# Graph network layer on one core: one gathered tile in 32 is built from SBUF columns instead

## The chip, the core and the metric

The kernel runs on one core of a Trainium2 chip. The core has five engines that run their own instruction streams side by side and wait for each other on semaphores: TensorE (PE, matrix products into PSUM banks), VectorE (DVE), ScalarE (ACT), GpSimd (POOL) and SyncE (SP, which only issues DMAs here). The metric is the time of one execution on the device in microseconds (us), the median of several runs.

## The reference

`x` holds 12500 nodes of 64 features. 200000 edges, sorted by `dst`, have a source and a destination node and 32 features each. What is computed:

```python
msg_in = concatenate([nodes[row], nodes[col], edge_features], axis=-1)   # 64 + 64 + 32
messages = relu(msg_in @ mW1 + mb1) @ mW2 + mb2                         # 128 hidden, 64 out
aggregated = segment_sum(messages, col, num_segments=12500)
upd_in = concatenate([nodes, aggregated], axis=-1)
update = relu(upd_in @ uW1 + ub1) @ uW2 + ub2
out = layernorm(x + update)                                             # over the 64 features
```

`row` is `src`, `col` is `dst`. All data are float32.

## The kernel before

**Tables.** The hidden layer of a message is a sum of three products, and two of them depend on a node alone. So TensorE first multiplies all nodes with the source rows of `mW1` (`src_table`, 12800 x 128, in DRAM) and with the destination rows plus `mb1` (`dst_table`, in DRAM). `xc` is a resident tile of [128, 12800]: its rows 0 to 63 hold `x` transposed, one node a column; its rows 64 to 127 later hold counts.

**Groups and laps.** The edges are worked off in tiles of 128, four tiles to a group of 512 (`TPG`), 391 groups, and `UNROLL` = 8 groups to a lap, `ITERS` = 49 laps. On each engine lap 0 and the last lap are written out, and between them runs a loop (L413, 25 laps), then a second loop (L418, 22 laps) in which each lap also does one of 25 chunks of the node update and the layer norm. `k` is the number of a group in its lap. For a group g:

- GpSimd (`gather`, L223) issues four indirect DMAs. Each fetches for the 128 edges of a tile the rows of `src_table` into `ag[:, k, ...]`, by the indices in `slot_idx`. It may run 8 groups ahead: it waits for `s_idx` of group g - 8.
- SyncE loads the features of the edges into rows 96 to 127 of `picks` (L232) and 96 rows of `dst_table`, a window from a base that it reads into a register, into `picked` (L238). Since the edges are sorted, the destinations of a group lie in such a window.
- VectorE makes the one-hot `oh` of each edge's place in the window two groups ahead (`one_hot`, L299), adds the gathered rows to the product (`add_source`, L312), copies the indices of group g + 8 into `slot_idx` (`next_indices`, L318), and adds the sums of group g - 2 into `agg_t` (L328) and the counts into `xc` (L329), at columns from a register.
- TensorE transposes the one-hot of group g + 1 (L247), multiplies `picks` with `picked` (`hidden`, L260), and sums the messages of group g - 1 by window place (`aggregate`, L270, L274).
- ScalarE copies the transposed one-hot of group g + 1 out of PSUM (L285) and applies the ReLU to `hid` (L291).

The window bases of a lap are loaded into registers once a lap by one load of 8 values on VectorE and one on SyncE (`window_bases`, L333). Its first element is 8i for SyncE and 8i - 2 for VectorE in lap i.

**What sets the order.** Each engine's instructions stand in the order in which they are written, k by k; semaphores that count groups tie the engines together. In `add_source` VectorE waits for three things, the first of which is the gathered rows:

```python
wait(dve, s_gathered[k], (lap + 1) * 16 * TPG - 16 * missing)
wait(dve, s_h, g + 1)
wait(dve, s_agg, g - 1)
```

In the laps of the second loop VectorE has steps of a chunk behind k = 1, 2, 5 and 6 (`dve_c2`, `dve_stack`, `dve_center`, `dve_variance`, `dve_normalize`), ScalarE at k = 3 and 6, TensorE at k = 2, 3 and 5. Ahead of the laps stands a prologue of some 100 us, in which the tables are made, and in which VectorE works out windows that SyncE stores to DRAM and loads back spread over the partitions.

Of the kernel before, what the change touches and what calls it, by code (L numbers as in the profile page):

```python
# [6 lines left out]
D = 64  # L7
# [31 lines left out]
TSTEPS = -(-BLOCKS // TB)  # L39
ASLOTS = UNROLL  # L40
# [6 lines left out]
def build(nc, x_rows, x_t, src_first, src_all, dst_groups, dst_tiles, edge_t,  # L47
# [3 lines left out]
    bf16 = mybir.dt.bfloat16  # L51
    ALU = mybir.AluOpType
# [6 lines left out]
    with ctx:  # L59
# [15 lines left out]
        lag_dram = dram("window_lag", (GROUPS,))  # L75
        agg_dram = dram("agg_rows", (AGG_ROWS, AGG_W))
# [46 lines left out]
        oh = sb("oh", [P, RING, TPG * WIN])  # L123
        hid = sb("hid", [P, 2, TPG * DH])
# [3 lines left out]
        dst_g_real = resid[0:GROWS, GPP * GE:2 * GPP * GE]  # L128
        base_all = resid[:, 2 * GPP * GE:2 * GPP * GE + GROUPS]
# [34 lines left out]
        s_flag = sem("s_flag")  # L164
        s_rel = sem("s_rel")
# [12 lines left out]
        s_window = [sem(f"s_window{i}") for i in range(RING)]  # L178
        s_oh = sem("s_oh")
# [34 lines left out]


# [35 lines left out]
        def hidden(pe, g, k, lap):  # L251
# [6 lines left out]
            wait(pe, s_pre, g - 1)  # L258
            for j in range(TPG):
                last = nc.tensor.matmul(ps_h[q][:, j * DH:(j + 1) * DH], picks[:, r, j * P:(j + 1) * P],  # L260
                                        picked[:, r, :], start=True, stop=True)
# [25 lines left out]
        def relu(g, k):  # L287
# [16 lines left out]
        def add_source(g, k, lap):  # L304
# [4 lines left out]
            wait(dve, s_gathered[k], (lap + 1) * 16 * TPG - 16 * missing)  # L309
# [240 lines left out]
        def general_vector():  # L550
            dve = nc.vector
            dst_table_stored(dve)
            dve.wait_ge(s_src, 16)
# [203 lines left out]
        def _(pool):  # L757
# [14 lines left out]
            def windowed():  # L772
                with pool.Fori(1, ITERS - 1) as i:  # L773
                    for k in range(UNROLL):
                        gather(pool, i * UNROLL + k, k)
                for g in range((ITERS - 1) * UNROLL, G_END):
                    gather(pool, g, g % UNROLL, min(TPG, T_END - g * TPG))
# [4 lines left out]
        def _(sp):  # L782
            sp.dma_start(slot_idx[:, :], src_first).then_inc(s_first, 16)
            sp.dma_start(dst_g, dst_groups).then_inc(s_dstg, 16)
            sp.dma_start(w_dst[:, :], mw1[D:2 * D, :]).then_inc(s_wdst, 16)
# [9 lines left out]
            sp.wait_ge(s_scratch, 64)  # L795
# [62 lines left out]
        def _(act):  # L858
# [11 lines left out]
            def windowed():  # L870
                dst_table_stored(act)
                copy_oh(0, 0)

                def lap(i, c):
                    for k in range(UNROLL):
# [7 lines left out]
                        if exists(g):  # L883
                            relu(g, k)
# [193 lines left out]
```

## Time and profile before

| | |
|---|---|
| time, median of 3 runs | 2049.36 us (2049.04 to 2050.01) |
| profiled execution, its own time | 2048.59 us |
| span in its profile | 2046.8 us |
| busy: GpSimd / TensorE matmul / VectorE / ScalarE | 1480 / 1439 / 872 / 563 us |
| gathers | 1563, 946 ns each |
| laps of the first loop / of the second | 25 / 22 |

The span is the stretch that the profile covers; the 1.8 us between it and the execution's own time lie outside. The busy time of an engine is the sum of its instructions; its sequencer, which reads the instructions, works out addresses in registers, loads registers and issues DMAs, is shown apart, as DVEq, ACTq, POOLq and SPq, and isn't counted as busy. Idle time before an instruction is put down to what ended it, behind an arrow; "issue" stands for time in which the engine waited for nothing that the profile shows.

### The profile page before, as it was taken

How to read it: one execution, taken by the hardware profiler on the slowest of the kernel's cores; microseconds unless marked ns; L12 is line 12 of the kernel's file. 1: busy time of each engine (PE TensorE's matmuls, PEld its weight loads, DVE VectorE, ACT ScalarE, POOL GpSimd, SP SyncE). 2: the span in 40 equal slices, each digit the busy share in tenths (PEclk: the TensorE clock that was granted, in tenths of full speed). 3: DMA queues.
4: the chain of work that ended last, by engine and by line, in shares of the span. 5: the costliest groups of instructions: out<-in, count | busy, mean ns of one | idle time of the engine just before them, and what ended most of it. 6: DMA issues, size and time to landing. Idle time of an engine off the chain costs nothing.

```text
span 2046.8 us, 34700 instructions
## 1 busy us (share of the span) xinstructions
PE 1438.8 (70%) x10080; PEld 1316.0 (64%) x10080; DVE 871.9 (43%) x2220; ACT 562.8 (27%) x929; POOL 1480.1 (72%) x1572
## 2 busy tenths in 40 slices
PE   7986666776666766766677767677677767667675
PEld 7976666666656666665666656566566656566664
DVE  3353333333333343333333444445444444444444
ACT  2332222222222222222222333233333333333332
POOL 0567777777777777777777777777777777777774
PEclk9997777777787687778876878787888778877877
DMA  8732323322232233223222223233223322232321
GB/s 212 206 100 79 80 78 77 82 78 78 80 80 78 78 80 80 77 78 81 79 76 72 80 78 82 75 81 79 76 78 80 80 75 81 78 80 75 82 78 46
DMA packets 167585, 173.49 MB, mean 85 GB/s; under 512 B 65654, under 2 KB 129433, under 8 KB 167209
## 3 DMA queue, kind: packets, MB, share of 16 engines
q0 software_dynamic: 50016, 102.53, 19.4%
q1 hardware_dynamic: 104088, 63.37, 11.2%
q10 hardware_dynamic: 13458, 7.31, 1.6%
q8 instruction: 12, 0.20, 0.0%
q14 instruction: 11, 0.08, 0.0%
HBM read 156.74 MB, written 16.31 MB: 85 GB/s over the span
## 4 chain that ended last, share of the span: by engine, by line
POOL 68%; issue 24%; PE 5%; POOLq 1%; DMA 1%; DVE 0%; ACT 0%; SPq 0%; ACTq 0%; DVEq 0%
POOL ag L223 68%; PE bank L367 4%; DMA xc<-x_t 1%; PE bank L260 0%; POOLq L209 0%; PE bank L270 0%; POOLq L220 0%; POOLq L773 0%; PE bank L634 0%; DMA ag<-src_table,slot_idx 0%; DMA dst_table<-picks 0%; DMA picks<-edge_t 0%; PE bank L247 0%; PE bank L640 0%; PE bank L274 0%
## 5 line engine op out<-in xcount | busy, mean ns | idle before, releaser
L223 POOL DMA_INDIRECT ag<-src_table,slot_idx x1563 | 1479.1, 946 | 543.8 <-issue 485.3
L270 PE MATMUL bank<-oh,hid 128*128 128x96 f32 x3128 | 533.5, 326 | 414.2 <-DVE xc L329 370.5
L270 PEld LDWEIGHTS bank<-oh,hid 128*128 128x128 f32 x3128 | 479.9, 234 | 472.7 <-ACT hid L291 425.0
L312 DVE TENSOR_TENSOR hid<-bank,ag 128x512 f32<-128x512 f32 x391 | 270.3, 691 | 886.6 <-DMA ag<-src_table,slot_idx 751.0
L260 PE MATMUL bank<-picked,picks 128*128 128x128 f32 x3128 | 582.5, 345 | 3.7 <-DMA picks<-edge_t 3.1
L291 ACT ACTIVATE hid<-hid 128x512 f32<-128x512 f32 x391 | 245.7, 628 | 1164.8 <-DVE hid L312 1164.8
L260 PEld LDWEIGHTS bank<-picked,picks 128*128 128x128 f32 x3128 | 520.7, 252 | 6.9 <-issue 3.3
L285 ACT ACTIVATE picks<-bank 96x512 f32<-96x512 f32 x391 | 226.2, 579 | 181.8 <-PE bank L247 132.3
L299 DVE TENSOR_TENSOR oh<-iota,rel 128x384 f32<-128x384 f32 x391 | 218.0, 558 | 117.9 <-PE bank L274 61.1
L247 PE MATMUL bank<-ident_bf,oh 128*96 128x128 bf16 x1564 | 193.6, 260 | 53.2 <-DVE oh L299 52.6
L247 PEld LDWEIGHTS bank<-ident_bf,oh 128*96 128x96 bf16 x1564 | 147.4, 155 | 103.4 <-DVE oh L299 65.7
L274 PE MATMUL bank<-oh,ones_bf 128*128 128x96 bf16 x1564 | 156.5, 230 | 0.0
L274 PEld LDWEIGHTS bank<-oh,ones_bf 128*128 128x128 bf16 x1564 | 144.4, 123 | 1.2
L634 PE MATMUL bank<-agg_t,w_pad 128*128 (+2 forms) x50 | 50.5, 1119 | 90.3 <-DVE resid L655 90.3
L328 DVE TENSOR_TENSOR agg_t<-bank,agg_t 128x96 f32 x391 | 100.6, 257 | 15.6 <-PE bank L274 1.8
L329 DVE TENSOR_TENSOR xc<-bank,xc 64x96 f32 x391 | 102.2, 261 | 5.9 <-issue 0.5
L318 DVE COPY slot_idx<-src_idx 128x4 int32 (+1 forms) x384 | 66.0, 172 | 57.6 <-DVE hid L312 57.3
L634 PEld LDWEIGHTS bank<-agg_t,w_pad 128*128 128x128 f32 x50 | 12.7, 313 | 94.8 <-issue 89.3
L367 PE MATMUL bank<-w_src,xc 64*128 64x128 f32 x200 | 43.0, 418 | 12.3 <-DMA xc<-x_t 12.3
L367 PEld LDWEIGHTS bank<-w_src,xc 64*128 64x128 f32 x200 | 42.7, 330 | 12.3 <-issue 12.3
L640 PE MATMUL bank<-xc,u 128*128 (+2 forms) x50 | 27.4, 634 | 26.0 <-DVE xc L663 26.0
L367 PE MATMUL bank<-w_dst,xc 64*128 64x128 f32 x200 | 43.0, 418 | 0.8 <-ACT ag L378 0.8
(55 smaller groups left out, 349.4 us busy)
## 6 DMA issues: line engine op xcount, KB each, us to landing
picks<-edge_t SPq DMA_DIRECT2D x391, 64.0 KB
ag<-src_table,slot_idx POOLq DMA_INDIRECT x1563
picked<-dst_table SPq DMA_DIRECT2D x391, 48.0 KB
src_table<-ag SPq DMA_DIRECT2D x25, 256.0 KB, 3.5
dst_table<-picks SPq DMA_DIRECT2D x17, 256.0 KB, 2.6
xc<-x_t ACTq DMA_DIRECT2D x4, 800.0 KB, 16.0
resid<-x_rows SPq DMA_DIRECT2D x24, 128.0 KB
out<-resid ACTq DMA_DIRECT2D x24, 128.0 KB
```

Source lines behind the costliest of these rows:

```text
L223: pool.indirect_dma_start(out=ag[:, k, j * DH:(j + 1) * DH], out_offset=None, in_=src_table, in_offset=bass.IndirectOffsetOnAxis(ap=slot_i ...
L247: last = nc.tensor.matmul(ps_o[q][0:WIN, j * P:(j + 1) * P], half[:, j * WIN:(j + 1) * WIN], ident_bf[:, :], start=True, stop=True)
L260: last = nc.tensor.matmul(ps_h[q][:, j * DH:(j + 1) * DH], picks[:, r, j * P:(j + 1) * P], picked[:, r, :], start=True, stop=True)
L270: nc.tensor.matmul(ps_a[q][:, 0:WIN], hid[:, q, j * DH:(j + 1) * DH], oh[:, r, j * WIN:(j + 1) * WIN], start=(j == 0), stop=(j == TPG - 1))
L274: last = nc.tensor.matmul(ps_a[q][:, WIN:2 * WIN], ones_bf[:, :], half[:, j * WIN:(j + 1) * WIN], start=(j == 0), stop=(j == TPG - 1))
L285: act.activation(picks[0:WIN, r, :], ps_o[q][0:WIN, :], ACT.Copy).then_inc(s_oht, 1)
L291: act.activation(hid[:, q, :], hid[:, q, :], ACT.Relu).then_inc(s_relu, 1)
L299: dve.tensor_tensor(oh[:, r, :].rearrange("p (j w) -> p j w", w=WIN), iota[:, None, :].to_broadcast(grid), rel[:, ds(g * TPG, TPG)][:, :, ...
L312: dve.tensor_tensor(hid[:, q, :], ps_h[q][:, :], ag[:, k, :], ALU.add).then_inc(s_pre, 1)
L328: dve.tensor_tensor(to, ps_a[q][:, 0:WIN], to, ALU.add)
L329: dve.tensor_tensor(cnt, ps_a[q][D:P, WIN:2 * WIN], cnt, ALU.add).then_inc(s_added, 1)
L367: last = nc.tensor.matmul(banks[n % 4][:, b * DH:(b + 1) * DH], xc[0:D, at:at + P], w[:, :], start=True, stop=True)
```

## The change

Group k = 5 of each lap from 1 on loses the gather of its last tile. In its place the sources' columns of `x` are collected in SBUF: `own_x` is [64, 128], one edge a column. Of its 128 columns 16 are filled in each of the 8 groups before, from k = 5 of the lap ahead on: 8 by VectorE with `tensor_copy`, 8 by ScalarE with a copying activation. Each column is `xc[0:64, node]`, and `node` is in a register that one load of 8 values fills, from `own_row`, one partition of SBUF in which the sources of these tiles stand as 16-bit integers. TensorE multiplies `own_x` with the source weights into the same PSUM columns on top of the product of L260, once both engines have reported their columns. `add_source` of that group then adds 384 columns only, and the ReLU is two activations, one straight from PSUM. In the prologue the indices come in by a DMA, are cast by VectorE, stored to DRAM and loaded back into `own_row`.

```diff
+        def own_indices(eng, lap, at, n):
+
+            return nc.values_load_multi_w_load_instructions(
+                own_row[0:1, ds(lap * P + at, n)], engines=(eng,), min_val=0, max_val=N_NODES - 1,
+                skip_runtime_bounds_check_because="an index of a node")[1]
+        def own_part(k, lap):
+
+            return lap + (k >= OWN_K), (k - OWN_K) % UNROLL * OWN_N
+        def fills_own(lap):
+
+            return not isinstance(lap, int) or 0 < lap < ITERS
+        def own_columns_dve(k, lap):
+
+            dve = nc.vector
+            lap, at = own_part(k, lap)
+            if fills_own(lap):
+                for n, node in enumerate(own_indices(ET.DVE, lap, at, OWN_DVE)):
+                    last = dve.tensor_copy(own_x[:, at + n:at + n + 1], xc[0:D, ds(node, 1)])
+                last.then_inc(s_own_dve, 1)
+        def own_columns_act(k, lap):
...
+                for n, node in enumerate(own_indices(ET.Activation, lap, at, OWN_N - OWN_DVE)):
+                    last = act.activation(own_x[:, at + n:at + n + 1], xc[0:D, ds(node, 1)], ACT.Copy)
+                last.then_inc(s_own_act, 1)
...
+            if own:
+                pe.wait_ge(s_own_dve, lap * UNROLL)
+                pe.wait_ge(s_own_act, lap * UNROLL)
+                last = nc.tensor.matmul(ps_h[q][:, OWN_AT:], own_x[:, :], w_src[:, :], start=False, stop=True)
             last.then_inc(s_h, 1)
...
+            if has_own(k, lap):
+                act.activation(hid[:, q, OWN_AT:], ps_h[q][:, OWN_AT:], ACT.Relu)
+                act.activation(hid[:, q, 0:OWN_AT], hid[:, q, 0:OWN_AT], ACT.Relu).then_inc(s_relu, 1)
+                return
...
-            dve.tensor_tensor(hid[:, q, :], ps_h[q][:, :], ag[:, k, :], ALU.add).then_inc(s_pre, 1)
+            w = OWN_AT if has_own(k, lap) else TPG * DH
+            dve.tensor_tensor(hid[:, q, 0:w], ps_h[q][:, 0:w], ag[:, k, 0:w], ALU.add).then_inc(s_pre, 1)
...
-                        gather(pool, i * UNROLL + k, k)
+                        gather(pool, i * UNROLL + k, k, TPG - (k == OWN_K))
...
-            sp.wait_ge(s_scratch, 64)
+            sp.wait_ge(s_own_h, 1)
+            sp.dma_start(own_dram, own_h).then_inc(s_scratch, 16)
+            sp.wait_ge(s_scratch, 80)
+            sp.dma_start(own_row[:, :], own_dram.rearrange("(o t) e -> o (t e)", o=1)).then_inc(s_own_row, 16)
...
                         if exists(g):
-                            relu(g, k)
+                            relu(g, k, i)
+                        own_columns_act(k, i)
...
                             add_window(g - 2, (k - 2) % UNROLL, bases[k])
+                        own_columns_dve(k, i)
                         if c is not None:
                             if k == 1:
                                 dve_c2(c)
```

On VectorE, inside the first loop, a group ended before with the two adds of `add_window`, and the one-hot and `add_source` of the next group followed (ISA is a register operation of the sequencer, `oh` the one-hot, `hid` what goes into the ReLU):

```order
L328 ISA [waits s_added,s_agg]
L328 TENSOR_TENSOR agg_t<-bank,agg_t 128x96
L329 ISA
L329 TENSOR_TENSOR xc<-bank,xc 64x96
L299 ISA [waits s_agg]
L299 TENSOR_TENSOR oh<-iota,rel 128x384
L312 TENSOR_TENSOR hid<-bank,ag 128x512 [waits s_agg,s_h,s_gathered1]
```

In the changed kernel the same place reads as follows (L395 and L396 are the old L328 and L329); the last two rows stand seven times more before the one-hot, now L365:

```order
L395 ISA [waits s_added,s_agg]
L395 TENSOR_TENSOR agg_t<-bank,agg_t 128x96
L396 ISA
L396 TENSOR_TENSOR xc<-bank,xc 64x96
L234 ISA
L234 TENSOR_LOAD own_row
L256 ISA
L256 COPY own_x<-xc 64x1
```

So a load and 8 pairs of a register operation and a copy stand between a group's last add and the next one-hot, in every group.

On ScalarE, in the first loop, a group was the copy of the one-hot and the ReLU:

```order
L209 REGISTER_ALU
L285 ACTIVATE picks<-bank 96x512 [waits s_h,s_oht_mm]
L291 ACTIVATE hid<-hid 128x512 [waits s_pre]
L209 REGISTER_ALU
L285 ACTIVATE picks<-bank 96x512 [waits s_h,s_oht_mm]
```

Now, at k = 5, where the ReLU is split (the last two rows again stand seven times more):

```order
L225 REGISTER_ALU
L347 ACTIVATE picks<-bank 96x512 [waits s_h,s_oht_mm]
L354 ACTIVATE hid<-bank 128x128 [waits s_pre]
L355 ACTIVATE hid<-hid 128x384
L234 ISA
L234 TENSOR_LOAD own_row
L266 ISA
L266 ACTIVATE own_x<-xc 64x1
```

The next copy of a one-hot out of PSUM thus stands behind a load and 8 activations.

On TensorE, at k = 5 in the first loop, before:

```order
L260 MATMUL bank<-picked,picks 128x128 [waits s_window1,s_pre,s_edge1,s_oht]
L260 MATMUL bank<-picked,picks 128x128 x3
L270 MATMUL bank<-oh,hid 128x96 [waits s_added,s_relu]
L270 MATMUL bank<-oh,hid 128x96 x3
L274 MATMUL bank<-oh,ones_bf 128x96 x4
```

And after:

```order
L318 MATMUL bank<-picked,picks 128x128 [waits s_window1,s_pre,s_edge1,s_oht]
L318 MATMUL bank<-picked,picks 128x128 x3
L323 MATMUL bank<-w_src,own_x 128x128 [waits s_own_act,s_own_dve]
L332 MATMUL bank<-oh,hid 128x96 [waits s_added,s_relu]
L332 MATMUL bank<-oh,hid 128x96 x3
L336 MATMUL bank<-oh,ones_bf 128x96 x4
```

One matmul more, with a wait for both engines that fill `own_x`, ahead of the aggregation of the group before.

## Rows read from the trace of the kernel before

**Rows 1.** The page: chain that ended last by engine, the gathers' group.

```profile
POOL 68%; issue 24%; PE 5%; POOLq 1%; DMA 1%; DVE 0%; ACT 0%; SPq 0%; ACTq 0%; DVEq 0%
...
L223 POOL DMA_INDIRECT ag<-src_table,slot_idx x1563 | 1479.1, 946 | 543.8 <-issue 485.3
```

**Rows 2.** Timeline of GpSimd: start us, us, engine, line, instruction, idle before.

```profile
620.71 0.94 POOL L223 DMA_INDIRECT ag<-src_table,slot_idx  x1 [0.30 <-issue]
621.96 0.94 POOL L223 DMA_INDIRECT ag<-src_table,slot_idx  x1 [0.30 <-issue]
```

**Rows 3.** VectorE's loop branches: ns min/median/max, first to last start us.

```profile
L413 DVEq FUSED_REGOPS  x25: 85/85/85, 125.2 to 1071.8; - x25
...
L413 DVEq COMPARE_BRANCH  x25: 50/56/67, 152.7 to 1111.5; - x25
...
L418 DVEq COMPARE_BRANCH  x22: 50/56/69, 1152.1 to 1993.9; - x22
```

**Rows 4.** Line L312 in 140 to 1100, 1120 to 2000, 1994 to 2047 us.

```profile
  DMA ag<-src_table,slot_idx: 488.0, 192
...
  DMA ag<-src_table,slot_idx: 241.1, 134
  issue: 124.9, 42
...
  DMA ag<-src_table,slot_idx: 14.4, 6
```

**Rows 5.** Register loads of L333: whole run, prologue's end, last stretch.

```profile
L333 DVEq TENSOR_LOAD <-base_row x50: 529/1846/1865, 102.3 to 2029.1; - x50
L333 SPq TENSOR_LOAD <-base_row x49: 521/525/701, 102.2 to 1974.8; - x49
...
L333 DVEq TENSOR_LOAD <-base_row x1: 844/844/844, 102.3 to 102.3; - x1
...
L333 DVEq TENSOR_LOAD <-base_row x2: 529/1188/1847, 1994.0 to 2029.1; - x2
```

**Rows 6.** Timeline of VectorE: a lap's end, then a whole group.

```profile
671.96 0.26 DVE L329 TENSOR_TENSOR xc<-bank,xc 64x96 f32 x1
674.42 0.57 DVE L299 TENSOR_TENSOR oh<-iota,rel 128x384 f32<-128x384 f32 x1 [2.20 <-PE bank L274]
...
1025.39 0.69 DVE L312 TENSOR_TENSOR hid<-bank,ag 128x512 f32<-128x512 f32 x1 [2.93 <-DMA ag<-src_table,slot_idx]
...
1026.71 0.26 DVE L329 TENSOR_TENSOR xc<-bank,xc 64x96 f32 x1
1027.00 0.56 DVE L299 TENSOR_TENSOR oh<-iota,rel 128x384 f32<-128x384 f32 x1
```

**Rows 7.** Register operation ahead of that L329; small independent instructions in the prologue.

```profile
L329 DVEq FUSED_REGOPS  x1: 65/65/65, 1026.5 to 1026.5; - x1
...
15.18 0.15 DVE L924 TENSOR_TENSOR spread<-dst_mx,base_f 98x4 f32<-98x4 f32 x1
15.25 0.15 DVE L928 TENSOR_TENSOR lag<-lag_f,base_f 98x4 f32<-98x4 f32 x1
```

**Rows 8.** Groups of ScalarE, shapes kept apart: busy us, mean ns, idle before.

```profile
L291 ACT ACTIVATE hid<-hid 128x512 f32<-128x512 f32 x391 | 245.7, 628 | 1164.8 <-DVE hid L312 1164.8
L285 ACT ACTIVATE picks<-bank 96x512 f32<-96x512 f32 x391 | 226.2, 579 | 181.8 <-PE bank L247 132.3 <-DMA dst_table<-picks 30.0 <-DVE resid L713 19.2
...
L693 ACT ACTIVATE dst_i<-resid 128x128 f32<-128x128 f32 x1 | 0.3, 309 | 0.8 <-DVE resid L687 0.8
```

**Rows 9.** A matmul of 64 rows; VectorE's wait for its first bank.

```profile
L367 PE MATMUL bank<-w_src,xc 64*128 64x128 f32 x200 | 43.0, 418 | 12.3 <-DMA xc<-x_t 12.3
...
58.26 0.69 DVE L388 TENSOR_TENSOR picks<-bank,b_rows 128x512 f32<-128x512 f32 x1 [18.10 <-PE bank L367]
```

**Rows 10.** Lines L318 and L223, whole run: duration ns min/median/max.

```profile
L318 DVE COPY slot_idx<-src_idx x384: 169/170/394, 108.3 to 1993.5; 128x4 int32 x188, 128x4 int32<-128x4 int32 x4
...
L223 POOL DMA_INDIRECT ag<-src_table,slot_idx x1563: 940/944/1285, 59.4 to 2023.8; - x196
```

More of the change, by code:

```diff
@@ L39 @@
 TSTEPS = -(-BLOCKS // TB)
+OWN_K = 5
+OWN_N = P // UNROLL
+OWN_DVE = OWN_N // 2
+OWN_J = TPG - 1
+OWN_AT = OWN_J * DH
 ASLOTS = UNROLL
@@ L213, in upper_halves, with has_own, gathered_of @@
             return ap.bitcast(bf16).rearrange("p (n two) -> p n two", two=2)[:, :, 1]
+        def own_indices(eng, lap, at, n):
+            return nc.values_load_multi_w_load_instructions(
+                own_row[0:1, ds(lap * P + at, n)], engines=(eng,), min_val=0, max_val=N_NODES - 1,
+                skip_runtime_bounds_check_because="an index of a node")[1]
+        def has_own(k, lap):
+            return k == OWN_K and not (isinstance(lap, int) and lap == 0)
+        def own_part(k, lap):
[10 more added lines that the diff above has]
+        def own_columns_act(k, lap):
+            act = nc.scalar
+            lap, at = own_part(k, lap)
+            at += OWN_DVE
+            if fills_own(lap):
+                for n, node in enumerate(own_indices(ET.Activation, lap, at, OWN_N - OWN_DVE)):
+                    last = act.activation(own_x[:, at + n:at + n + 1], xc[0:D, ds(node, 1)], ACT.Copy)
+                last.then_inc(s_own_act, 1)
+        def gathered_of(k, lap):
+            return 16 * TPG + lap * 16 * (TPG - (k == OWN_K))
         def gather(pool, g, k, tiles=TPG):
@@ L258, in hidden @@
             wait(pe, s_pre, g - 1)
+            own = has_own(k, lap)
             for j in range(TPG):
                 last = nc.tensor.matmul(ps_h[q][:, j * DH:(j + 1) * DH], picks[:, r, j * P:(j + 1) * P],
-                                        picked[:, r, :], start=True, stop=True)
+                                        picked[:, r, :], start=True, stop=not (own and j == OWN_J))
+            if own:
+                pe.wait_ge(s_own_dve, lap * UNROLL)
+                pe.wait_ge(s_own_act, lap * UNROLL)
+                last = nc.tensor.matmul(ps_h[q][:, OWN_AT:], own_x[:, :], w_src[:, :], start=False, stop=True)
             last.then_inc(s_h, 1)
@@ L285, in copy_oh, with relu @@
             act.activation(picks[0:WIN, r, :], ps_o[q][0:WIN, :], ACT.Copy).then_inc(s_oht, 1)
-        def relu(g, k):
+        def relu(g, k, lap):
             act = nc.scalar
@@ L308, in add_source @@
             missing = G_END * TPG - T_END if isinstance(g, int) and g == G_END - 1 else 0
-            wait(dve, s_gathered[k], (lap + 1) * 16 * TPG - 16 * missing)
+            wait(dve, s_gathered[k], gathered_of(k, lap) - 16 * missing)
             wait(dve, s_h, g + 1)
             wait(dve, s_agg, g - 1)
-            dve.tensor_tensor(hid[:, q, :], ps_h[q][:, :], ag[:, k, :], ALU.add).then_inc(s_pre, 1)
+            w = OWN_AT if has_own(k, lap) else TPG * DH
+            dve.tensor_tensor(hid[:, q, 0:w], ps_h[q][:, 0:w], ag[:, k, 0:w], ALU.add).then_inc(s_pre, 1)
         def next_indices(g, k):
```

22 lines of the change are left out of this document (20 added, 2 removed).

## The prediction

> **What bounds the kernel now.** Read the page's chain that ended last first: GpSimd holds 68% of it and "issue" another 24%, and GpSimd's gathers are busy for 1479 of 2046.8 us and preceded by 485 us of "issue", 0.3 us each [rows 1]. The timeline of GpSimd shows the gathers at an even pitch, 620.71, 621.96, with no wait on anybody [rows 2]. The laps of VectorE take (1111.5 - 152.7) / 24 = 39.95 us without the update and (1993.9 - 1152.1) / 21 = 40.09 us with it [rows 3]; a lap of 8 groups has 32 gathers, and 39.95 / 32 = 1.248 us is the pitch of the timeline. So today's lap is a lap of gathers.
>
> The second question is how far behind the next engine is. The idle time of VectorE before `add_source` (L312) is the slack: in 24 laps without the update it waits 488.0 us for gathered rows, 20.3 us a lap; in 22 laps with it 241.1 us, 11.0 us a lap, and another 124.9 us that no gather ended ("issue": waits inside the chain of the update, which stay) [rows 4]. Taking one gather out of a lap is worth 1.248 us; whatever VectorE gets in return has to fit into these two numbers.
>
> **What is removed.** One gather in each of the laps 1 to 48: 48 x 1.248 = 59.9 us, if GpSimd stayed the bound. That is the most that the change can give: 2048.6 - 59.9 = 1989 us. A lap of gathers becomes 31 x 1.248 = 38.7 us.
>
> **What VectorE gets.** After the window add of every group (L396 in the new file) it loads 8 node numbers into registers and copies 8 columns, each from an address in a register. So 8 loads and 64 copies a lap, 384 groups in all (3 in lap 0, 8 in each of the laps 1 to 47, 5 in lap 48).
>
> *The load.* VectorE has a load of 8 registers already, once a lap (`window_bases`, L333): 50 of them, median 1846 ns, and the only shorter ones are a load of 6 registers (844 ns) and one of 2 (within 529 to 1847 ns, so 529) [rows 5]. The sequencer does nothing else meanwhile: at a lap's end L329 is over at 672.22 and the next one-hot starts at 674.42, where it follows 0.03 us behind in the middle of a lap [rows 6]. SyncE loads the same 8 numbers in 525 ns [rows 5]. The two differ in the engine and in where the load begins: element 8i for SyncE, 8i - 2 for VectorE. The new loads are VectorE's, begin at a multiple of 16 and read 2-byte numbers, so both ends are possible: 0.52 us and 1.85 us. I take 1.85: same engine, same number of registers, and its median and its longest are 19 ns apart; the 6 registers at 844 ns, which begin at element 0, are what speaks against it.
>
> *The copies.* Each has a register operation in front of it, 65 ns for the one that stands before L329 today, and small independent instructions start 70 ns behind each other although each runs 150 ns [rows 7]. So 0.06 + 0.07 = 0.13 us a column, 1.04 us for 8. Lower bound 0.07 (register operations cost nothing), upper bound 0.20 (a copy runs 0.17 us, as L318 does [rows 10], and the next waits for its end and 0.03 us).
>
> *The sum for one group*: 0.07 us register operation ahead of the load, 1.85 load, 1.04 columns, 0.13 for the register operation and dispatch of the following one-hot, which today hides beside L329, and minus 0.30 us, since the sequencer is done with L329 (1026.5 + 0.065) well before the engine is (1026.97) and starts the load meanwhile [rows 6, 7]: 2.79 us. A lap: 8 x 2.79 = 22.3 us against a slack of 20.3 and 11.0 us. It doesn't fit. VectorE becomes the bound:
> - a lap without update: 39.95 - 20.3 + 22.3 = 41.95 us (from the other side: a group without waits on others runs from 1025.39 to 1027.00 + 0.56, 2.2 us [rows 6], 8 x (2.2 + 2.79) + 2.2 for the lap's own load = 42.1);
> - a lap with update: 40.09 - 11.0 + 22.3 = 51.4 us.
>
> **What else moves.** ScalarE gets the same load and 8 activations. Its two instructions of a group take 579 + 628 ns, an activation of 128 columns 309 ns [rows 8], of which some 0.1 us are the columns (628 - 309 = 319 ns for 384 more); with 1.85 us for the load and 0.2 us a column a group is 1.2 + 1.85 + 1.6 = 4.65 us, under VectorE's 2.2 + 2.79 = 4.99, so it hides behind VectorE even at that upper end. TensorE gets one matmul a lap (64 rows, at 418 ns for one of its two passes [rows 9], so under 0.9 us) that waits for the columns of the group before; VectorE's next one-hot (0.56 us) runs meanwhile, so at most 0.3 us of a lap is exposed, and I count nothing. ScalarE's split ReLU costs one more start, some 0.2 us, off the path. In the prologue SyncE waits for one more small store before it loads the window tables, and VectorE reads them; VectorE stands idle there for 18 us until TensorE has its first bank [rows 9], which covers it. GpSimd's wait for free indices is 8 groups behind and costs nothing while gathers are not late; once VectorE is the bound, GpSimd waits there, which is where the removed 60 us go.
>
> **The sum.** Lap 0 ends at 125.2 us on VectorE [rows 3], plus 3 x 2.79 = 8.4: 133.6. Then 25 x 41.95 = 1048.8, 0.9 for the entry into the second loop, 22 x 51.4 = 1130.8. The last lap and the tail took 2046.8 - 1993.9 = 52.9 us; 5 x 2.79 = 14.0 us more stand against 14.4 us of waits for gathers in it [rows 4], so 52.9 again. Total 2367.0 us of span; the profiled execution is 1.8 us longer than its span (2048.59 to 2046.8) and 0.8 us under the median, so about **2369 us**, 15.6% slower.
>
> **A rule against the rows.** The trace has loads at 0.52 and 1.85 us [rows 5]. The Trainium skill ("Runtime: NRT & Kernel Launch", section Instruction fetch mechanics) says that a register load (the runtime's own, from HBM) costs about 200 ns for each register even in bulk; 8 would be an estimated 1.6 us, which is nearer to VectorE's row and disagrees with SyncE's, and with 1.6 the sum above would come to some 2275 us, still slower.
>
> **Rivals.**
> (a) *The load is as quick as SyncE's (0.52 us).* A group costs 0.07 + 0.52 + 1.04 + 0.13 - 0.30 = 1.46 us, a lap 11.7 us. That fits into 20.3 (the lap is then the gathers' 38.7) and nearly into 11.0 (40.09 - 11.0 + 11.7 = 40.8): -1.25 x 25 + 0.7 x 22 = -16, so 2033 us, and 1989 us if the columns take 0.07 each as well. This is the side on which the kernel gets faster; with columns at 0.13 it decides at a load of about 0.6 us. For it: SyncE's 49 loads. Against it: none of VectorE's is that short with over 2 registers.
> (b) *The load is in between, 1.0 us*, as a line through VectorE's 529 ns for 2 and 844 ns for 6 registers gives for 8. A group costs 1.94 us, a lap 15.5: still 38.7 without the update, but 44.6 with it: 2048.6 - 31 + 22 x 4.5 + 4 = 2121 us, slower.
> (c) *The columns don't overlap* (0.20 each): 0.56 us more in each of 384 groups, 2369 + 215 = 2584 us.
> (d) *The copies stop GpSimd.* VectorE's small copy L318 runs 384 times beside the gathers; its median is 170 ns, its shortest 169, and the gathers stand at 940 to 944 ns in half their records [rows 10]: no sign that either waits. If each of the 8 copies held a gather for the 0.15 us it runs, the pitch would be 1.248 + 2 x 0.15 = 1.55 us, the lap without the update 31 x 1.55 = 48.0, and the total 2369 + 25 x 6 = 2520 us. The Trainium skill ("SBUF — State Buffer", Who interferes with whom) has this rule: a copy of VectorE between SBUF tensors in a 2-port mode and a GpSimd instruction shut each other out completely; by it the time is this rival's, and the trace shows no sign of it for L318.
> (e) *Nothing of the kind: 48 gathers less and all the rest hidden*, 1989 us. It needs (a) and the cheap columns together and is counted with (a).
>
> **How the numbers follow.** Chances: forecast 0.61 (load 1.6 to 2.1 us), (a) 0.16, (b) 0.14, (c) 0.06, (d) 0.03. The forecast's own range comes from the load at 1.6 (384 x 0.25 = 96 us less), from the columns at 0.10 (384 x 0.24 = 92 less) and, upward, from the 0.30 us of overlap that may not be there (384 x 0.30 = 115 more): 2185 to 2485 us. The range of 8 in 10 takes in (b) and the slower half of (a), whose forecast is 2033: 2025 to 2485. It leaves out the quick half of (a), (c) and (d). What a measurement can tell from no change here is about 0.2%, 4 us; (a) lies on both sides of it where the load is near 0.6 us. Faster 0.15, same 0.04, slower 0.81.
>
> **What would show it.** In the profile after: the register loads that the changed kernel adds on VectorE, with their duration (1.85 us confirms the main term, 0.5 us overturns it); idle time of GpSimd that VectorE's `slot_idx` copy ends, beside the even 0.3 us of "issue" that is all it has now; VectorE's wait for gathers in L379 gone to nearly nothing in both loops; the laps at 42 and 51 us by the loop's branches; copies of 64x1 starting 0.13 us apart. The forecast is wrong if the loads are short, or if ScalarE or TensorE, not VectorE, is what the others wait for in the laps with the update: then the second number, 51.4, is too low, since waits of one engine within the update's chain would add up with those of the other.

## The result, and the profile after

The changed kernel takes 2390.3 us (median of 4 runs, 2387.3 to 2392.8), the kernel before 2049.7 us in the same session (2049.0 to 2050.1): a ratio of 1.166, 95% interval 1.164 to 1.168. The forecast was 2369 us. The profiled execution took 2387.3 us, 2385.5 of them span. The runs of experiments 5 and 6 were taken on two other chips, on which the kernel before itself takes 2672 and 2670 us: no conclusion on the time of a kernel is drawn from them, only on the duration of single instructions.

The page of the changed kernel, first the busy time of each engine, then the two groups that answer to [rows 1] and to the added columns:

```profile
PE 1600.0 (67%) x10176; PEld 1449.1 (61%) x10176; DVE 1232.8 (52%) x5293; ACT 924.3 (39%) x4050; POOL 1464.9 (61%) x1524
...
L280 POOL DMA_INDIRECT ag<-src_table,slot_idx x1515 | 1463.9, 966 | 861.4 <-issue 405.1
L256 DVE COPY own_x<-xc 64x1 f32 x3072 | 366.7, 146 | 653.8 <-issue 653.8
```

48 gathers are gone (1515 for 1563), and GpSimd's idle time has grown from 543.8 to 861.4 us. VectorE is busy for only 52% of the span, but before its column copies it stands "idle" for 653.8 us: that is not a wait for anybody, it is the register load, which the page doesn't count as busy. One line of the register loads, one of the copies, from their line views (duration ns min/median/max):

```profile
L234 ACTq TENSOR_LOAD <-own_row x384: 1707/1716/2078, 118.8 to 2358.4; - x192
L234 DVEq TENSOR_LOAD <-own_row x384: 1823/1828/2189, 119.1 to 2357.6; - x192
...
L256 DVEq FUSED_REGOPS  x3072: 46/46/53, 120.9 to 2360.2; - x192
```

384 loads of 1.83 us on VectorE, 384 of 1.72 us on ScalarE. A group of VectorE, to be held against [rows 6] (timeline; start us, us, instruction):

```profile
700.69 0.26 DVE L396 TENSOR_TENSOR xc<-bank,xc 64x96 f32 x1
702.65 0.95 DVE L256 COPY own_x<-xc 64x1 f32 x8 [1.70 <-issue]
703.59 0.56 DVE L365 TENSOR_TENSOR oh<-iota,rel 128x384 f32<-128x384 f32 x1
704.18 0.69 DVE L379 TENSOR_TENSOR hid<-bank,ag 128x512 f32<-128x512 f32 x1
```

From L396 to the next one-hot it is 2.90 us; it was 0.29 us (1026.71 to 1027.00). So a group costs VectorE 2.61 us more. There is no idle time before L379: the gathered rows are there. The line view of L379 gives 3.9 us of waits in 192 groups of the first loop (for L323, the added matmul), where [rows 4] had 488.0 us for gathers. The loops' branches on VectorE, to be held against [rows 3]:

```profile
L480 DVEq FUSED_REGOPS  x25: 85/85/85, 131.2 to 1121.0; - x25
L480 DVEq COMPARE_BRANCH  x25: 50/56/67, 172.3 to 1162.0; - x25
...
L485 DVEq COMPARE_BRANCH  x22: 50/56/69, 1216.7 to 2332.5; - x22
```

The first loop (L480) takes (1162.0 - 172.3) / 24 = 41.24 us a lap, before 39.95; the second (L485), which carries the update, (2332.5 - 1216.7) / 21 = 53.13 us, before 40.09. The tail is 2385.5 - 2332.5 = 53.0 us as it was. Of the 339 us of span, 6 come from lap 0 (131.2 for 125.2), 45 from the first loop (125.2 to 1111.5 before, 131.2 to 1162.0 now; 14 of them from its first lap, which took 27.5 us and now takes 41.1 like the rest) and 288 from the second (to 1993.9 before, to 2332.5 now).

### The profile page after: what moved, and what is told of

The parts are those of the page before. It is cut to its first block and busy times, and to the rows that moved or that the text cites. A ratio compares the mean times of both kernels' runs of the same rounds, so it can differ in the third digit from the quotient of the medians.

```text
span 2385.5 us, 48801 instructions
## 1 busy us (share of the span) xinstructions
PE 1600.0 (67%) x10176; PEld 1449.1 (61%) x10176; DVE 1232.8 (52%) x5293; ACT 924.3 (39%) x4050; POOL 1464.9 (61%) x1524
## 5 line engine op out<-in xcount | busy, mean ns | idle before, releaser
L280 POOL DMA_INDIRECT ag<-src_table,slot_idx x1515 | 1463.9, 966 | 861.4 <-issue 405.1
L256 DVE COPY own_x<-xc 64x1 f32 x3072 | 366.7, 146 | 653.8 <-issue 653.8
L332 PE MATMUL bank<-oh,hid 128*128 128x96 f32 x3128 | 599.8, 356 | 102.6 <-ACT hid L357 80.0
L332 PEld LDWEIGHTS bank<-oh,hid 128*128 128x128 f32 x3128 | 565.1, 271 | 131.5 <-ACT hid L357 117.7
L318 PE MATMUL bank<-picked,picks 128*128 128x128 f32 x3128 | 610.9, 357 | 22.7 <-ACT picks L347 16.4
L318 PEld LDWEIGHTS bank<-picked,picks 128*128 128x128 f32 x3128 | 541.1, 260 | 34.1 <-issue 24.5
L266 ACT ACTIVATE own_x<-xc 64x1 f32 x3072 | 344.2, 193 | 489.1 <-issue 489.1
L357 ACT ACTIVATE hid<-hid 128x512 f32<-128x512 f32 x343 | 215.3, 628 | 494.7 <-DVE hid L379 492.7
L379 DVE TENSOR_TENSOR hid<-bank,ag 128x512 f32<-128x512 f32 (+1 forms) x391 | 263.7, 674 | 198.7 <-issue 174.1
L365 DVE TENSOR_TENSOR oh<-iota,rel 128x384 f32<-128x384 f32 x391 | 219.6, 562 | 126.4 <-issue 68.1
L323 PE MATMUL bank<-w_src,own_x 64*128 64x128 f32 x96 | 30.3, 407 | 126.6 <-DVE own_x L256 125.7
L395 DVE TENSOR_TENSOR agg_t<-bank,agg_t 128x96 f32 x391 | 100.9, 258 | 14.2 <-issue 3.5
L396 DVE TENSOR_TENSOR xc<-bank,xc 64x96 f32 x391 | 102.0, 261 | 5.4
L708 PE MATMUL bank<-xc,u 128*128 (+2 forms) x50 | 44.5, 990 | 87.5 <-DVE xc L731 87.5
L323 PEld LDWEIGHTS bank<-w_src,own_x 64*128 64x128 f32 x96 | 18.7, 242 | 136.9 <-DVE own_x L256 136.9
```

The lines of the kernel that those rows point to most:

```text
L256: last = dve.tensor_copy(own_x[:, at + n:at + n + 1], xc[0:D, ds(node, 1)])
L266: last = act.activation(own_x[:, at + n:at + n + 1], xc[0:D, ds(node, 1)], ACT.Copy)
L280: pool.indirect_dma_start(out=ag[:, k, j * DH:(j + 1) * DH], out_offset=None, in_=src_table, in_offset=bass.IndirectOffsetOnAxis(ap=slot_i ...
L332: nc.tensor.matmul(ps_a[q][:, 0:WIN], hid[:, q, j * DH:(j + 1) * DH], oh[:, r, j * WIN:(j + 1) * WIN], start=(j == 0), stop=(j == TPG - 1))
L365: dve.tensor_tensor(oh[:, r, :].rearrange("p (j w) -> p j w", w=WIN), iota[:, None, :].to_broadcast(grid), rel[:, ds(g * TPG, TPG)][:, :, ...
L379: dve.tensor_tensor(hid[:, q, 0:w], ps_h[q][:, 0:w], ag[:, k, 0:w], ALU.add).then_inc(s_pre, 1)
```

## The experiments

The question on top: is it VectorE's time, as forecast, and of that the load? The rival: the gathers, since the changed kernel waits for them by other counts and gathers three tiles of a group instead of four. Then: why does one load of 8 registers take 0.52 us and another 1.83?

**1. Eight kinds of load in the kernel before.** Each group of the first loop gets one more load on VectorE and on ScalarE, and one copy that uses its last value.

```
+ load_a8(i): base_row[0:1, ds(i * UNROLL, 8)]          L344
+ load_m8(i): base_row[0:1, ds(i * UNROLL - 2, 8)]      L347
+ load_a6(i): base_row[0:1, ds(i * UNROLL, 6)]          L350
+ load_a4(i): base_row[0:1, ds(i * UNROLL, 4)]          L353
+ load_a2(i): base_row[0:1, ds(i * UNROLL, 2)]          L356
+ load_a1(i): base_row[0:1, ds(i * UNROLL, 1)]          L359
+ load_h8(i): row16[0:1, ds(i * 2 * UNROLL, 8)]         L362
+ load_s8(i): base_row[0:1, 8:16]                       L365
```

> The kernel before with one register load more in each group of the first loop, on VectorE and on ScalarE, each followed by one small copy that uses its last value: 8 int32 from element 8i, 8 int32 from 8i-2, 4, 2, 1 int32 from 8i, 8 int16 from a multiple of 16, 6 int32 from 8i, 8 int32 from a fixed element. What decides how long a load of 8 takes on VectorE? If it is the start (theory S), the aligned int32 load takes 0.5 to 0.9 us and 8i-2 takes 1.85, and ScalarE shows the same split. If it is the engine and the number of registers (theory N, a cost per register), all loads of 8 take about 1.85 us on VectorE, 4 about 1.1, 2 about 0.6, 1 about 0.35. If the 2-byte type alone is slow (theory T), the int32 loads are short and the int16 one takes 1.83 us. Time of the whole: these loads cost VectorE some 8 x 1.6 = 13 us a lap against 20 us of slack, so 2049 us under N and less load under S; any rise over 0.5% would mean that loads also slow GpSimd.

The line views, VectorE's loads and one of ScalarE:

```profile
L344 DVEq TENSOR_LOAD <-base_row x25: 594/598/607, 127.8 to 1100.6; - x25
L347 DVEq TENSOR_LOAD <-base_row x25: 1854/1859/1872, 130.5 to 1105.8; - x25
L350 DVEq TENSOR_LOAD <-base_row x25: 825/828/837, 148.5 to 1130.8; - x25
L353 DVEq TENSOR_LOAD <-base_row x25: 344/347/352, 134.4 to 1110.7; - x25
L356 DVEq TENSOR_LOAD <-base_row x25: 535/539/549, 137.2 to 1115.9; - x25
L359 DVEq TENSOR_LOAD <-base_row x25: 310/314/317, 139.9 to 1120.9; - x25
L362 DVEq TENSOR_LOAD <-base_row x25: 1830/1834/1852, 143.8 to 1126.0; - x25
...
L344 ACTq TENSOR_LOAD <-base_row x25: 537/550/565, 127.3 to 1100.1; - x25
```

The engine makes little difference (598 and 550 ns); the type and the start decide, so theories S and T hold together and N falls. One int32 costs 314 ns, two 539, but four from a multiple of 16 bytes 347 and eight 598. The same eight int32 from 8 bytes before such a multiple cost 1859, and eight int16 from a multiple of 16 bytes 1834. All of it agrees, to some 30 ns, with one reading: a load takes its int32 in fours as long as each four begin at a multiple of 16 bytes, and anything else value by value, at (1834 - 314) / 7 = 217 ns each. Six are then four together and two alone, 347 + 2 x 225 = 797 ns, measured 828 (225 ns is what the second of two costs). So the 844 ns that the prediction took for "6 registers" is such a sum, and SyncE's 525 against VectorE's 1846 in [rows 5] is the start (8i against 8i - 2), not the engine. The Trainium skill ("Runtime: NRT & Kernel Launch", section Instruction fetch mechanics) gives some 200 ns for each register of the runtime's own loads from HBM even in bulk: the loads value by value, here from SBUF, agree (217 ns), the ones in fours (87 ns a register for four, 75 for eight) don't.

The run took 2072.3 us against 2050.3 (one run), though the loads, 6.9 us a lap on VectorE, fit almost three times into its slack of 20.3. Experiment 4 comes back to that.

**2. The gather isn't left out.** The fourth tile of the group k = 5 of each lap is gathered too, and not used; the waits count as in the kernel before. Everything else stays.

```
- return 16 * TPG + lap * 16 * (TPG - (k == OWN_K))
+ return (lap + 1) * 16 * TPG
...
- gather(pool, i * UNROLL + k, k, TPG - (k == OWN_K))
+ gather(pool, i * UNROLL + k, k)
...
```

> The changed kernel, but all 32 tiles are gathered as before, and the gathered rows of the 32nd tile are not used. If VectorE is the bound (my theory), the gather given back costs nothing: 2390 us within 0.3%. If the time of the changed kernel still hangs on GpSimd (rival), it rises by up to 60 us, to 2450.

2389.3 us (4 runs; 1.166 times the kernel before, 1.164 to 1.168), against 2390.3 for the changed kernel: the 48 gathers are worth nothing. GpSimd has 1563 gathers again and still stands idle until VectorE's indices are written:

```profile
L280 POOL DMA_INDIRECT ag<-src_table,slot_idx x1563: 938/944/1338, 58.8 to 2327.2; - x196
...
  DVE slot_idx L385: 343.8, 262
```

In the changed kernel that row is 399.4 us in 296 waits: 56 of the 60 us that were taken off GpSimd went into this wait.

**3. One column of eight.** The loads stay, each engine copies one column a group; the other 14 of 16 are left out and hold zeros, so the product of the tile is made with a mostly empty own_x.

```
- for n, node in enumerate(own_indices(ET.DVE, lap, at, OWN_DVE)):
+ for n, node in list(enumerate(own_indices(ET.DVE, lap, at, OWN_DVE)))[:1]:
...
- for n, node in enumerate(own_indices(ET.Activation, lap, at, OWN_N - OWN_DVE)):
+ for n, node in list(enumerate(own_indices(ET.Activation, lap, at, OWN_N - OWN_DVE)))[:1]:
```

> The changed kernel with its loads, but only the first of the 8 columns of each group is copied on VectorE and on ScalarE; the other columns hold zeros. A group gets 1.83 + 0.2 - 0.3 us and one column: 1.8 us, 14.5 us a lap. Without the update that fits (38.7 us a lap); with it 29.1 + 14.5 + 3 us = 46.6 where the changed kernel has 53.1. Sum: 2049 - 31 + 22 x 6.5 = 2160 us; 2095 if the 3 us that the changed kernel's update laps take above my sum come from the columns. If a load hides beside other work better than I think, it is at 2000.

```profile
L480 DVEq COMPARE_BRANCH  x25: 50/56/67, 163.2 to 1106.6; - x25
...
L485 DVEq COMPARE_BRANCH  x22: 50/56/69, 1154.2 to 2090.8; - x22
```

2139.7 us (1.044, 1.042 to 1.045), between the two times expected. The first loop is down to 39.31 us a lap, the second to 44.60. Seven columns less are 7 x 0.115 = 0.81 us a group, 6.4 us a lap. The second loop gains 8.5 us by it, 2.1 more than VectorE spends on the columns; experiment 7 shows where they come from.

**4. No load.** The copies take their addresses from the loop's counter, so no index is read, and the columns are those of other nodes.

```
- return nc.values_load_multi_w_load_instructions(
-     own_row[0:1, ds(lap * P + at, n)], engines=(eng,), ...)[1]
+ return [lap * P + (at + m) for m in range(n)]
```

> The changed kernel without the register loads on VectorE and ScalarE: the address of a column comes from the lap's register and a constant, so each column still has its register operation and its copy, but the columns are those of other nodes. If the load is the main cost (my theory), VectorE gets 8 columns x 0.115 us and about 0.2 us more a group, 9 us a lap, which fits into 20.3 and 11.0 us: the laps are the 38.7 us of 31 gathers, total 1990 to 2010 us. If the columns or the coupling of three engines are what costs (rival), it stays over 2200 us.

```profile
POOL 68%; issue 23%; PE 6%; DMA 1%; POOLq 1%; DVE 1%; ACT 0%; SPq 0%; DVEq 0%; ACTq 0%
...
L278 POOL DMA_INDIRECT ag<-src_table,slot_idx x1515 | 1474.2, 973 | 529.3 <-issue 467.4
```

2030.6 us (0.990, 0.9885 to 0.9918). Without the load 360 us are gone, the chain is GpSimd's again, and this kernel, which doesn't compute the right columns, is 1% faster than the kernel before. Load and columns don't add up: all columns without the load are worth -20 us against the kernel before, the loads with one column +89, both together +341, since each alone fits, or nearly, into the slack of the laps. But it is slower than the 1990 to 2010 us expected, and this is the second place where laps of gathers are too long: the loops' branches give 40.04 and 39.23 us for 31 gathers, where 31 x 1.248 is 38.7. That is experiment 1's riddle again. The mean gather has grown from 946 to 973 ns, and the timeline says which:

```profile
635.40 0.94 POOL L278 DMA_INDIRECT ag<-src_table,slot_idx  x1 [0.30 <-issue]
636.51 0.56 DVE L363 TENSOR_TENSOR oh<-iota,rel 128x384 f32<-128x384 f32 x1 [2.45 <-issue]
636.64 1.24 POOL L278 DMA_INDIRECT ag<-src_table,slot_idx  x1 [0.30 <-issue]
```

This gather starts while the one-hot runs and ends 0.81 us after the one-hot's end (637.07 to 637.88) instead of 0.94 after its own start. All 142 gathers of this run that start 0.045 to 0.37 us into a one-hot are held like it and take 1.006 us or more. Over this run the gathers are 44 us longer than 944 ns each, in the kernel before 4 us, and the difference is what 2030.6 lies above 2050.3 - 59.9 = 1990.4. In the kernel before VectorE waits for the gathers in L312, which keeps its one-hot mostly at a fixed place between two of them, and only 20 gathers are over a microsecond; here 160 are. The loads of experiment 1 loosen the same lock: 136 gathers are over a microsecond there, and all are 27 us longer instead of 4, which is about its 22 us. The column copies do nothing of the kind: none of the 163 gathers that start inside one is over a microsecond. At 638.72 to 639.59 eight copies run across the start of a gather of 0.94 us.

```profile
638.72 0.87 DVE L254 COPY own_x<-xc 64x1 f32 x8
639.44 0.94 POOL L278 DMA_INDIRECT ag<-src_table,slot_idx  x1 [0.30 <-issue]
```

**5. The one-hot reads iota from PSUM.** Theory: the gather is held because the one-hot has both its inputs in SBUF. The Trainium skill has that rule ("SBUF — State Buffer", Who interferes with whom): such an instruction contends with a GpSimd instruction that reads SBUF; one with at most one SBUF input, outside VectorE's 2-port modes, doesn't. The edit, here on the kernel of experiment 4, and once more in experiment 6:

```
- iota = sb("iota", [P, WIN])
+ iota = banks[6][:, 0:WIN]
```

> The kernel without register loads (e3), with the one-hot's iota moved from SBUF into the PSUM bank that nothing uses, so that the one-hot has one SBUF input instead of two. The kernel without loads had laps of 40.04 us without the update, where 31 gathers at 1.248 us are 38.7; its gathers that start while a one-hot runs take 1.25 to 1.34 us instead of 0.94. If it is the one-hot that holds them through its second SBUF input (my theory), they are all back at 0.94 us here, the laps at 38.7, and the total near 1995 us. If it is VectorE's column copies that hold them (rival, the fourth of the prediction), the gathers stay as they are, and the total stays at 2030.

The time, 2720.3 us against 2672.3 for the kernel before, says nothing on it, for the reason given with the result. The gathers say it: their mean is 946 ns for 973, at the same number of columns. The last two kernels of experiment 6, on one chip, differ in nothing but the place of iota, and there the count is clean: of the gathers that start 0.045 to 0.37 us into a one-hot, all 126 take over 1 us with iota in SBUF (`e11_first_loop_int32`), and of 110 with iota in PSUM (`e12_first_loop_int32_psum`) none takes more than 0.947. One of the latter, 0.17 us into the one-hot:

```profile
485.16 0.56 DVE L371 TENSOR_TENSOR oh<-bank,rel 128x384 f32<-128x384 f32 x1 [2.28 <-remote]
485.33 0.94 POOL L286 DMA_INDIRECT ag<-src_table,slot_idx  x1 [0.30 <-issue]
```

The trace of experiment 4 has a pair of its own in the update: of the 16 gathers that start inside `resid<-resid,stat` (L753, both inputs in SBUF) 14 take over 1 us, of the 17 that start inside `resid<-bank,resid` (L746, one input in PSUM, the same 128x256) none. The mechanism is shown, and the rule agrees with it; what moving iota would give in time isn't shown.

**6. The tile left out in the first loop alone, with int16 and with int32 indices, and with iota in PSUM.** The laps with the update gather all 32 tiles again; own_row then needs to hold some half as many numbers and is kept as int32 in two of the three. Each was run in two sessions, on two chips.

```
- with pool.Fori(1, ITERS - 1) as i:
+ with pool.Fori(1, UPD_LAP) as i:
...
+ with pool.Fori(UPD_LAP, ITERS - 1) as i:
+     for k in range(UNROLL):
+         gather(pool, i * UNROLL + k, k)
...
- own_row = sb("own_row", [1, ITERS * P], i16)
+ own_row = sb("own_row", [1, (UPD_LAP + 1) * P], i32)
```

> The changed kernel with the own tile in the 25 laps of the first loop only; the laps with the update gather all 32 tiles and have no columns. VectorE is still the bound of the first loop (41.2 us a lap), 50 us behind the kernel before at its end, of which GpSimd's lead of 6 more groups gives back some 30: about 2070 us. If the second loop's cost in the changed kernel came from something left behind by the first, it would be well above.

> The same with the node numbers as int32, 8 from a multiple of 16 elements. By the measured loads this one takes 0.6 us instead of 1.83, so a group costs VectorE 1.4 us more than before instead of 2.6, 11 us a lap against 20.3 of slack: the first loop is bound by 31 gathers again. Without any hold of GpSimd 38.7 us a lap and 2018 us in all; with gathers held by one-hots as in the kernel without loads (1.35 us a lap) 2050. If the type of the number were not what decides the load, 2070 as with int16.

> The same with the iota in PSUM. If the one-hot's second SBUF input is what holds the gathers, the first loop has laps of 38.7 us and the total is 2049 - 31 = 2018 us, faster than before by 1.5%. Rival: no effect of the iota's place, same time as the run with int32 alone.

> The changed kernel with the tile taken from the gathers in the first loop alone (groups 4 to 203); the laps with an update gather all 32 tiles, as before. Theory (the load bounds): the first loop keeps its 41.2 us a lap against 39.95, 24 laps x 1.29 = 31 us, and the second loop is back at 40.1, so 2078 to 2090 us. Rival (the load is hidden in the first loop and only the update's chain pays): 2040 to 2055 us.

> As the run before it, but the indices lie in own_row as int32, so that 4 of them begin at a multiple of 16 bytes: the two loads of 8 cost about 0.60 us on VectorE and 0.55 on ScalarE in place of 1.83 and 1.72. Theory (type and start decide, and VectorE's added time is 1.4 us a group): VectorE's chain fits under the gathers; 31 gathers a lap x 0.946 + 0.98 x 8 would be 37.2 us a lap, but VectorE's own sum is about 40.0 - 8 x (2.61 - 1.24) = 30.3 us of the old cover, so the lap ends between 39 and 40.3, some gathers being held by the one-hot: 2030 to 2055 us. Rival (the type is nothing): the loads stay at 1.8 us and the time equals that of the int16 run.

> As the int32 run, with iota in a PSUM bank, so that the one-hot reads one of its two inputs from PSUM. If a gather that starts inside a one-hot is held because both instructions read SBUF, then all gathers take 0.944 to 0.950 us again and the time falls by 20 to 35 us against the int32 run, to 2010 to 2025 us; if the one-hot has nothing to do with it, the time stays within 5 us of the int32 run.

Ratios to the kernel before beside them: first session (2672.3 us) 1.007, 1.008 and 1.011; second session (2670.1 us) 1.009 (1.006 to 1.013), 1.010 (1.007 to 1.012) and 1.014 (1.010 to 1.017). None of the expected times came out, neither 2010 to 2090 us nor the order of the three. In the second session the loads are what the theory says in the changed kernel's own place; int16 first, then int32:

```profile
L236 DVEq TENSOR_LOAD <-own_row x203: 1421/1828/1844, 163.9 to 1494.6; - x102
...
L236 DVEq TENSOR_LOAD <-own_row x203: 594/597/720, 164.0 to 1496.8; - x102
```

VectorE's idle time before its columns falls from 354.1 to 106.9 us, and GpSimd's mean gather with iota in PSUM from 967 to 945 ns. And the time doesn't move, since another thing bounds the laps there: by VectorE's branches a lap of the first loop takes 52.7, 52.8 and 53.0 us in the three kernels, a lap of the second, with a whole update more to do, 52.8, 52.5 and 52.7. The timeline of the int32 run shows ScalarE, VectorE and TensorE standing still together and going on at one moment, after waits that end by something that has no record ("remote"):

```profile
2102.59 0.59 ACT L353 ACTIVATE picks<-bank 96x512 f32<-96x512 f32 x1 [8.02 <-remote]
2102.61 0.56 DVE L371 TENSOR_TENSOR oh<-iota,rel 128x384 f32<-128x384 f32 x1 [7.14 <-remote]
2102.81 0.32 SPq L301 DMA_DIRECT2D picked<-dst_table  x1
```

The counts that ScalarE and VectorE wait for here are TensorE's; they rise at 2102.5, while the last matmul that the trace shows before it ends at 2098.9. What held them isn't settled. Whether a version with int32 in the first loop beats the kernel before on the chips of the other runs stays open: what is known is that the load of 1.83 us is 0.60 there, and that a lap can fall no lower than 31 x 1.248 = 38.7 us, 25 x 1.25 = 31 us in all, of which held gathers take a part.

**7. VectorE's columns alone.** The second loop's lap of 53.13 us is 3.1 us over what VectorE's gain explains (40.09 - 11.0 + 8 x 2.61 = 50.0). ScalarE's part is left out: no loads, no columns, half of own_x stays empty.

```
- for n, node in enumerate(own_indices(ET.Activation, lap, at, OWN_N - OWN_DVE)):
-     last = act.activation(own_x[:, at + n:at + n + 1], xc[0:D, ds(node, 1)], ACT.Copy)
- last.then_inc(s_own_act, 1)
+ pass
...
- pe.wait_ge(s_own_act, lap * UNROLL)
```

> The changed kernel without ScalarE's eight columns: ScalarE neither loads indices nor copies, and the other half of own_x stays zero, so those 8 of 64 columns x 2 of the tile's x are left out. VectorE loads and copies as before. Theory one: the 3 us by which a lap with an update is longer than the sum of what VectorE gained (8 x 2.61 + 29.1 = 50.0 against 53.13 measured) come from ScalarE's columns, which stand before its hid activation: then a lap with an update takes 50 to 51.4 and the time is 2320 to 2355 us. Theory two: they come from VectorE's own columns standing between its steps of the update: then the lap stays at 53 and the time within 2380 to 2392 us. The first loop is bound by VectorE alone in both: 41.1 to 41.4 per lap.

```profile
L477 DVEq COMPARE_BRANCH  x25: 50/56/67, 172.8 to 1165.5; - x25
...
L482 DVEq COMPARE_BRANCH  x22: 50/56/69, 1220.3 to 2336.1; - x22
```

2387.6 us (2 runs; 1.163, 1.159 to 1.168), laps of 41.36 and 53.13 us. Theory one falls: ScalarE's 384 loads and 3072 activations cost nothing that shows. The extra comes with VectorE's own part, and the waits of the second loop show where most of it sits: us in total, times, longest. First before (1152.1 to 1993.9 us), then the changed kernel (1216.7 to 2332.5), 21 laps each:

```profile
DVE hid L312 <- issue: 118.9, 40, 4.1
...
PE bank L640 <- DVE xc L663: 25.0, 21, 1.4
```

```profile
DVE hid L379 <- issue: 158.6, 42, 4.1
...
PE bank L708 <- DVE xc L731: 81.4, 21, 4.3
```

Two groups of a lap wait here for TensorE, at k = 2 and k = 3; the profile writes "issue", since it is the sequencer that waits, and the wait ends with TensorE's L318. At k = 2 VectorE's mean wait is as it was, 3.91 us for 3.95. At k = 3 it is 3.64 for 1.89: this is 1.7 of the 3.1 us. (The rows above count two of the 42 waits before as waits for a gather, so the mean is taken lap by lap from the trace.) TensorE's work ahead of it is the same in both kernels: a product of the update (L640, now L708), the transposes, and the eight matmuls of L260, now L318. Here it is in one lap, before and then changed:

```profile
1530.35 1.10 PE L640 MATMUL bank<-xc,u 128*128 x2 [1.20 <-DVE xc L663]
1531.51 1.11 PE L260 MATMUL bank<-picked,picks 128*128 128x128 f32 x8
1532.71 0.69 DVE L312 TENSOR_TENSOR hid<-bank,ag 128x512 f32<-128x512 f32 x1 [1.90 <-issue]
```

```profile
1505.92 2.05 PE L708 MATMUL bank<-xc,u 128*128 x2 [3.73 <-DVE xc L731]
1508.18 2.02 PE L318 MATMUL bank<-picked,picks 128*128 128x128 f32 x8
1510.30 0.69 DVE L379 TENSOR_TENSOR hid<-bank,ag 128x512 f32<-128x512 f32 x1 [3.92 <-issue]
```

The same matmuls take nearly twice as long, because the granted clock of TensorE is 0.50 from 1505.9 to 1510.3 and was 1.00 from 1530.35 to 1532.7: the lower and the upper of its two levels, 1.2 and 2.4 GHz. From the start of that product to VectorE's add it is 2.36 us in each of the 21 laps before, and 3.6 to 4.4 us in each of the 21 now. With one column (experiment 3) it is 2.36 us in 19 of 21 laps, which is most of the 2.1 us that the lap gained there beyond the columns; without ScalarE's part it is 3.5 to 4.4 us. Before that product TensorE stands waiting for VectorE's step (L663, now L731), 0.6 to 1.4 us before, 3.3 to 4.3 now, since the load and the columns stand ahead of that step in VectorE's order. With one column the wait is as a rule 3.4 us and the clock stayed up all the same, so the wait alone does not tell when the clock falls; what does isn't shown.

Of the other 1.4 us a lap, 0.3 is idle time ahead of the columns beyond that of the first loop (291.4 us in 21 laps for 325.0 in 24), 0.2 are L379's waits for L323 and 0.2 are before the one-hot (51.9 us for 46.8 in 21 laps). The last 0.7 isn't placed. A version with the update's step written ahead of the load and the columns was not run.

## Why the prediction was right, and where it wasn't

*Which engine bounds.* Right, and shown: GpSimd did, VectorE does. No wait for gathers is left in L379 in either loop, GpSimd waits for VectorE's indices, and with the gathers put back the time is the same.

*The load.* 1.85 us forecast, 1.83 measured: 384 x 1.83 = 703 us of VectorE's time, of which 360 reach the end. The choice between the two rows of [rows 5] was right, but its reason (same engine, same number) was wrong: the engine is worth 8%. What decides was also in those rows, as "where the load begins"; and what put the new loads, which do begin at a multiple of 16, on the slow side is their 2-byte type, of which the prediction only said that it differs.

*The columns.* 0.13 us forecast, 0.115 measured (0.95 us for 8), since the register operation takes 46 ns and not 65. With it the group is 2.61 us for 2.79.

*The lap without update.* 41.95 forecast, 41.24 measured, partly by two errors against each other: with 2.61 the same sum gives 40.5, and 0.7 us of the lap are waits that the sum left out. Of these 0.16 are L379's for the added matmul, which was counted at nothing with 0.3 as the bound, and 0.3 the wait at the lap's own load, which reads 2.5 us (60.1 in 24) for 2.2. That the forecast came so near to the total, 0.9% below, has to do with luck: the first loop was forecast 18 us too long and the second 39 too short.

*The lap with update.* 51.4 forecast, 53.13 measured: the term that was mis-sized, by 22 x 1.7 = 38 us. The prediction let the 124.9 us of "issue" in the update's chain [rows 4] stand as they were; they grew by 1.7 us a lap, since TensorE, whose work is the same, does its stretch at k = 3 at half the clock (experiment 7). That TensorE's clock could move was no term of the sum. The prediction had named a wait for TensorE or ScalarE as what would make 51.4 too low; it is TensorE, not ScalarE. Together: -2.4 us for lap 0, -18 for the first loop, +39 for the second, which is 2385.5 of span for the 2367 forecast. (The lower end of the forecast's own range, 2369 - 96 - 92, is 2181 and not 2185; nothing hangs on it.)

*Rivals.* (a), a load at SyncE's price, has an answer in experiment 1: such a load exists on VectorE, at 598 ns, for int32 from a multiple of 16 bytes; it was not what the change writes. (a) and (e) put the kernel with quick loads at 1989 to 2033 us; with no load at all it takes 2030.6, the held gathers included, so the lower end was out of reach. (b) fell with the line through 529 and 844 ns, which are two kinds of access and no line. (c): the columns overlap, 0.115 us apart at 0.146 each. (d) was argued from the wrong number of its row. Copies don't hold a gather, as said; but another VectorE instruction does. The median of 944 ns in [rows 10] says that most gathers were not held in that order of events, not that nothing can hold them; the longest in the same row, 1285 ns, was one of 19 that started inside a one-hot and were held.

## What to carry over

- Registers loaded in a loop are a cost of the sequencer that no busy share shows: look for "issue" ahead of the instruction that uses them and for the load's own line. Keep indices as int32 and let each group of four begin at a multiple of 16 bytes; in this case that is 0.60 us for 1.83.
- Work put on an engine with slack costs nothing only if it fits into the slack of the lap that has least of it (11.0 us here, not 20.3).
- When a wait in a chain of two engines grows, look at the durations behind the wait too: here TensorE stood longer, and the same matmuls behind it then ran at half the clock (4.4 us for 2.36).
- A lock step between two engines can hide a conflict: when work is added that loosens it, look at the durations on the other engine, not only at its waits.

## What the hardware showed that was not expected

- A register load on VectorE costs 347 ns for four int32 from a multiple of 16 bytes and 598 for eight, but 539 for two, 1834 for eight int16 and 1859 for eight int32 8 bytes off: as if fours that begin at such a multiple were fetched in one piece and everything else value by value.
- An indirect gather that starts 0.045 to 0.37 us into a one-hot with two SBUF inputs (0.56 us long) ends 0.81 to 0.83 us after it in all 142 cases of experiment 4, up to 0.4 us late (in no run over 1338 ns, for 944); with one of the inputs in PSUM it isn't held.
- Eight copies of one column by register addresses take 0.95 us on VectorE and 0.89 on ScalarE, and ScalarE's eight with their load cost this kernel no time.
- The granted clock of TensorE decides 2 us of a lap: one stretch of the same matmuls takes 2.36 us at 1.00 and 4.38 at 0.50.
- On two chips all versions that ran there, the one before too, took 2670 to 2720 us; the three of experiment 6 had laps of 52.5 to 53.0 us whatever they contained. Which wait sets these is not known.
